# Three chunks of C instead of four, and four buffers of scanned states instead of three, in a four-layer sequence kernel

## The reference

```python
dA = exp(delta[..., None] * A)                 # per channel and state
dBu = delta[..., None] * Bm[:, :, None, :] * u[..., None]
h = dA_t * h + dBu_t                            # over 256 steps
y = einsum('ben,bn->be', h, C_t)                # sum over the 16 states
```

## Time and profile before

| what | value |
|---|---|
| median of 3 runs | 3858.66 us |
| all three runs | 3858.66, 3845.4, 3859.24 us |
| the profiled execution | 3851.72 us |
| its span, first to last instruction | 3850.0 us |
| mean granted TensorE clock in it | 0.947 |
| instructions | 64705 |
| product L684, 1536 times | 1296 ns mean |
| scan L669, 1536 times | 1211 ns mean |
| transposes L565, 6144 times | 279 ns mean |

### The profile page before, as it was taken

How to read it: one execution, slowest core, us unless ns; L and a number is a source line. 1 busy time by engine, 2 the same in 40 slices (tenths; PEclk the granted TensorE clock), 3 DMA queues, 4 the chain that set the end, 5 groups by cost and what they waited for, 6 DMA issues and landing times.

```text
span 3850.0 us, 64705 instructions
## 1 busy us (share of the span) xinstructions
PE 3267.6 (85%) x22078; PEld 2693.0 (70%) x22078; DVE 2824.3 (73%) x3590; ACT 2918.2 (76%) x6624; POOL 2854.6 (74%) x3087
## 2 busy tenths in 40 slices
PE   4577788888888899888888999888888999887876
PEld 2456677777777778777777777777777777775643
DVE  0467778788787878788787878788787878784621
ACT  1568778887888788887888888888878888885522
POOL 0387989888787888888787888888787888882500
PEclk9799999999999999999999999999999999998876
DMA  4112222222221222222122222222222222221100
GB/s 164 45 55 78 76 70 78 72 65 79 61 80 60 76 65 68 74 64 79 57 75 64 78 65 68 73 64 82 58 74 65 78 65 66 72 67 35 42 2 10
DMA packets 140808, 257.09 MB, mean 67 GB/s; under 512 B 15905, under 2 KB 33313, under 8 KB 140081
## 3 DMA queue, kind: packets, MB, share of 16 engines
q1 hardware_dynamic: 140482, 252.95, 21.5%
HBM read 233.16 MB, written 5.05 MB: 62 GB/s over the span
## 4 chain that ended last, share of the span: by engine, by line
PE 42%; ACT 23%; DVE 12%; issue 8%; POOL 7%; DMA 2%; SPq 0%; DVEq 0%; POOLq 0%; ACTq 0%
PE ps_b L565 8%; PE ps_y L593 8%; ACT decay L630 8%; POOL g L684 5%; DVE hst L669 5%; PE ps_v L756 5%; ACT dbut L640 4%; PE ps_x L762 3%; PE ps_x L756 3%; PE ps_x L1265 3%; POOL dbut L649 2%; PE ps_x L1290 2%; ACT pT L1344 2%; DMA rows_bc<-mod_rows 2%; PE ps_x L765 2%
## 5 line engine op out<-in xcount | busy, mean ns | idle before, releaser
L684 POOL TENSOR_TENSOR g<-hst,c_bc 128x512 f32<-128x512 f32 x1536 | 1989.7, 1296 | 592.3 <-PE ps_y L593 410.0
L669 DVE TENSOR_TENSOR_SCAN hst<-decay,ps_b 128x512 f32<-128x512 f32 x1536 | 1831.6, 1211 | 502.4 <-PE ps_b L565 212.7
L630 ACT ACTIVATE decay<-delta,acoef 128x256 f32<-128x256 f32 x3072 | 1376.7, 498 | 7.3 <-DVE hst L669 6.7
L565 PE MATMUL ps_b<-ident,dbut 128*128 128x128 f32 x6144 | 956.0, 279 | 284.7 <-DVE hst L669 161.3
L649 POOL TENSOR_TENSOR dbut<-dut,bcm 128x256 f32<-128x256 f32 x1536 | 972.4, 633 | 201.7 <-ACT dut L855 201.7
L565 PEld LDWEIGHTS ps_b<-ident,dbut 128*128 128x128 f32 x6144 | 715.7, 143 | 367.2 <-issue 227.6
L593 PE MATMUL ps_y<-ident,g 128*128 128x128 f32 x6144 | 953.3, 279 | 7.4 <-POOL g L684 4.5
L593 PEld LDWEIGHTS ps_y<-ident,g 128*128 128x128 f32 x6144 | 752.4, 144 | 139.0 <-issue 41.7
L640 ACT ACTIVATE dbut<-dut,bcm 128x256 f32<-128x256 f32 x1536 | 766.7, 500 | 54.1 <-PE ps_b L565 50.2
L1290 PE MATMUL ps_x<-qT,kT 18*128 18x256 f32 x1024 | 160.1, 434 | 16.6 <-ACT pT L1344 15.7
L1344 ACT ACTIVATE pT<-ps_x 128x1024 f32<-128x1024 f32 x128 | 129.3, 1010 | 52.4 <-PE ps_x L1300 45.4
(11 more groups left out here) (192 smaller groups left out, 4082.3 us busy)
## 6 DMA issues: line engine op xcount, KB each, us to landing
c_bc<-c_rows SPq DMA_DIRECT2D x768, 256.0 KB, 3.2
rows_bc<-mod_rows SPq DMA_DIRECT2D x16, 384.0 KB, 4.5
weights<-in_weights_dram SPq DMA_DIRECT2D x1, 5792.0 KB
ada_w<-in_ada_w_dram SPq DMA_DIRECT2D x1, 5120.0 KB
x<-in_x_dram SPq DMA_DIRECT2D x16, 256.0 KB, 4.1
x0p<-x SPq DMA_DIRECT2D x16, 256.0 KB, 2.3
xr<-x SPq DMA_DIRECT2D x16, 256.0 KB, 3.6
x<-x SPq DMA_DIRECT2D x16, 256.0 KB, 2.6
```

The lines of the kernel that those rows point to most:

```text
L565: last = nc.tensor.matmul(ps_b[:, u % 2, e * T + t * P:e * T + (t + 1) * P], dbut[:, u % NDBU, t, e * P:(e + 1) * P], ident[:, :], is_tran ...
L630: last = nc.scalar.activation(decay[:, u % (DA_AHEAD + 2), e, :], delta[s][:, eb, :], ACT.Exp, scale=acoef[:, s, eb, n:n + 1])
L669: nc.vector.tensor_tensor_scan(line(hst[:, u % NHST, :, :].rearrange("p e t -> p (e t)")), line(decay[:, u % (DA_AHEAD + 2), :, :].rearran ...
L684: nc.gpsimd.tensor_tensor(g[:, u % NG, :, :], hst[:, u % NHST, :, :], c_bc[:, k % NCB * CHUNK + n % CHUNK, :].unsqueeze(1) .broadcast_to([ ...
```

## The change

The ring `c_bc` gets three chunks, the ring `hst` four buffers. A chunk takes 2 KB per partition, and so does a buffer of `hst`, so the sum of SBUF stays the same. The lead of the C loads, (NCB - 1) * CHUNK, goes from six units to four, and the scan of unit u waits for the product of unit u - 4 instead of u - 3. TICKS, the number of ticks over which every engine's program is written out, grows by 224.

```diff
-NCB = 4
+NCB = 3
 LAST = B
-NDBU, NHST, NG, NPT = 4, 3, 3, 2
+NDBU, NHST, NG, NPT = 4, 4, 3, 2
...
-        TICKS = BASE[LAST + 2] + 2 * DRAIN
+        TICKS = BASE[LAST + 2] + 4 * DRAIN
```

## The result

The changed kernel takes 3997.76 us (median of 4 runs, 3989.96 to 4008.42); the kernel before beside it 3853.11 us. The ratio is 1.0379, 95% interval 1.0344 to 1.0414: slower by 145 us where 98 were forecast, and above the range that ended at 3978.

A forecast was written before the change was run, and what follows sets the result against it. Taken as bound: a coupled pipeline of four engines waiting through short rings, none full. 14 x 3.6 + 13 x 4.1 = 103.7 us lost, 6 gained: 3851.72 + 103.7 - 6 = 3949.4 us; range 3875 to 3978.

The forecast's parts named there:

- What bounds the kernel: Whole kernel: four engines in a coupled pipeline wait for one another through short rings; TensorE busy 85%, none full.
- blocks X and Y: SyncE's waits at L995 (X, tick 77) and L1414 (Y, tick 6) hold back C chunks, 14 and 13 times.
- TICKS and instructions at 0: Build loops and instruction streams: longer loops emit nothing, same DMAs, products and scans in the same order; 0 us.
- The ends of the blocks don't move, and each DMA goes when it went before: SyncE's queue: both long waits end as before; each C load issues at its old time, carrying an earlier chunk.
- Block X at 3.6 us: At L995: product 82 stalls 5.65 us instead of 1.57, product 84 comes 3.6 us later, 14 times; bounds 3.1 to 4.1.
- Block Y at 4.1 us: At L1414: product 12 starts late, scan 18 comes 4.1 us later, 13 times; bounds 2.2 to 4.8.
- The late product: GpSimd's product 12, waiting for its C chunk at L1414, delays transposes and then scan 18 by 4.1 us.
- The fourth scanned-state buffer at 6 us: VectorE's scans (L669) wait less for products: 6 us gained, bounds 0 and 48.7.
- The sum: Whole kernel: 3851.72 + 103.7 - 6 = 3949.4 us.
- Partial recovery: Rival: other waits of the period absorb half the delay; 3898 us, chance 0.11.
- Compounding: Rival: a delay uncovers one more SyncE wait per period, losing 1.8 us each; 3976 us, chance 0.07.

The follow-up runs named there:

- Moving the two places: Changed kernel with SyncE's two blocking waits (L995, L1414) placed behind the work they wait for: 3830.56 us, ratio 0.9944.
- The run with Y moved: Changed kernel with only SyncE's wait for the layer 3 mask (L1414) moved to ticks 14 and 16: 3892.88 us, ratio 1.0097.
- moving both places there: Kernel before, old rings, with SyncE's same two blocking waits placed behind the work they wait for: 3840.65 us, ratio 0.997.
- Y alone: Changed kernel with only SyncE's wait at L995 moved, to tick 84, the L1414 wait left in place: 3931.65 us, ratio 1.0196.
- the extra transposes: Changed kernel plus 40 identity transposes on TensorE at unit 16 of periods 4 to 15 and once more: 3958.11 us, ratio 1.0303.
- the moved kernels: Both SyncE waits moved, in the changed kernel and in the kernel before: 3830.56 us with changed rings, 3840.65 us with old rings.
- an earlier issue: Changed kernel with both SyncE waits moved, next sequence's row loads issued three units earlier, second l0_mx wait at 87: 3779.81 us.

## Why the prediction was wrong

The direction, the mechanism and both places were right; the size was not. By its own steps:

- *What bounds the kernel; blocks X and Y.* Right. Moving the two places removes every chunk wait but the start-up one, and 167 us with them.
- *TICKS and instructions at 0.* The engines' instruction counts are those of before, and the ring of C alone, with the old TICKS, loses as much. TICKS was not tried alone.
- *The ends of the blocks don't move, and each DMA goes when it went before.* Right: SyncE waits 193.5 and 149.0 us there, for 193.9 and 148.9, and the stalls are 5.63 and 4.62 us in the period read, 137.6 us in all for 142.
- *Block X at 3.6 us.* The run with Y moved holds X alone: 4.5 us per block. The small stalls of the kernel before are in this too; moving both places there gave 15.9 us (3856.51 less 3840.65) over 27 blocks, 0.6 us each. So X grew by 3.9 us: about right, 4 us too little over 14 blocks. The traces agree: in periods 2 to 14 the stretch from the transposes of unit 80 to those of unit 94 grows by 3.9 us on average.
- *Block Y at 4.1 us.* This is the step that failed. It grew by 7.7 us on average in the traces (6.9 in the period read), and Y alone costs 7.8 per block in the times, 7.2 without the 0.6 of before: 40 to 47 us too little over 13 blocks. The term that was missing is TensorE's clock. The prediction put TensorE's work behind the stall at the durations and distances of before (the 6.28 us from unit 16 to unit 18); but TensorE stands idle for 4.55 us, and then works at half clock. That costs 3.3 us per block where the extra transposes prevented it, 43 us over 13, and the times bear out 29 to 40. The late product by itself is nearly right: 4.4 us with the clock held, 0.3 above the 4.1 that were taken.
- *The fourth scanned-state buffer at 6 us.* The forecast size can't be told from the 10 us between the moved kernels; the reason holds, since 42 us of waits removed gave at most about that.
- *The sum.* With the sizes of the runs, 14 x 3.9 + 13 x 7.2 = 148 us, less up to 10 for the buffer: 138 to 148, where 145 were measured. With the 7.7 of the traces the first sum is 155, where the span grew by 149.2 us. The forecast of 97.7 lacked some 40 us in block Y, nearly all of it the clock, and 4 in block X. These sizes are known to a few us at best, since medians of one kernel differ by as much.
- *The rivals.* Partial recovery did not happen: the delays added up block by block. Compounding in the sense of a further uncovered wait of SyncE did not happen either (27 waits, all at X or Y), but the rival had the right sign: a stall did cost more than the late product, by the clock. The range did not hold it, because both ends were built from durations at full clock.

## What to carry to other kernels

When a ring that is filled by an in-order queue gets shorter, look for what else stands in that queue: the lead has to cover its longest block as well as the transfer. Place a blocking wait behind the work it waits for, so that the queue never stands; here this was worth 167 us in the changed kernel and 12 to 16 us in the kernel before, and an earlier issue another 51. When a stall on another engine leaves TensorE without work for several microseconds, price what it does afterwards at the durations of the lower clock too, and put that into the upper bound.

## What the runs showed of the hardware

Behind an idle stretch of 4.55 us TensorE had a granted clock of 0.51 for 5.8 us, although it was busy 5.80 of them. The length of the idle stretch alone does not tell whether the clock falls. Behind block X just ahead of that block Y the transposes took 0.63 us after 3.36 us of idle time, so the clock had not fallen; behind block X a period earlier they took 1.08 us after 3.28:

```profile
1811.27 1.08 PE L565 MATMUL ps_b<-ident,dbut 128*128 128x128 f32 x4 [3.28 <-issue]
...
2041.21 0.63 PE L565 MATMUL ps_b<-ident,dbut 128*128 128x128 f32 x4 [3.36 <-issue]
```

In the changed kernel the clock falls behind 12 of the 14 blocks X, in the kernel before behind one. It costs little there: the stretch from unit 80 to unit 94 takes 30.9 and 31.2 us in the two periods without a fall, and 31.0 to 32.5 in periods 2 to 14 with one.

Work without any use, 40 transposes of an identity matrix put into an idle stretch, kept the clock at 1.00 in 11 of 12 blocks Y and made the stalled kernel 29 to 40 us faster; the same work cost 52 us where there was no stall.
